# Two graph layers and two feed-forward blocks on one core: GpSimd waits for its gathers after every sixteenth

## The reference

```
h = x @ w_nbr;  agg = segment_sum(edge_weight * h[src], dst)      # first layer
x = x + agg + x_norm @ w_own + bias
x = x + mixture(x_norm)          # router, best 2 of 8 experts, gelu MLP 256 -> 1024 -> 256
for i in range(3):               # three convolutions
    h = x @ W[i];  h = segment_sum(h[src] * norm, dst) + b[i]
    x = relu(layernorm(h) * gamma[i] + beta[i])
x = x + attention_over_slices(x_norm)
```

## Time and profile before

| | us |
|---|---|
| median of 3 runs | 3794.12 (3790.35 to 3794.98) |
| profiled execution, span from first to last instruction | 4365.6 |
| prologue, to the first gather | 60.8 |
| gathers of the first layer, first to last start | 60.8 to 1212.5 |
| gathers of the three passes, first to last start | 2395.6 to 4183.6 |
| TensorE busy | 3253.1 (75%) |
| GpSimd busy | 2531.6 (58%) |
| VectorE, ScalarE busy | 1790.8 (41%), 1496.2 (34%) |

### The profile page before, as it was taken

The page is one execution under the profiler, slowest core; times in us unless marked ns, Lnnn a source line. Parts: engine busy times, 40 slices in busy tenths (PEclk is TensorE's granted clock), DMA queues, the critical chain, the costliest instruction groups (busy, mean ns, idle before and its releaser), DMA issues. The chain is left out here.

```text
span 4365.6 us, 47498 instructions
## 1 busy us (share of the span) xinstructions
PE 3253.1 (75%) x15077; PEld 2484.5 (57%) x15077; DVE 1790.8 (41%) x5335; ACT 1496.2 (34%) x2892; POOL 2531.6 (58%) x2604
## 2 busy tenths in 40 slices
PE   1455565555446989988886798987989868999868
PEld 1344444444335777776764576655666645666547
DVE  4355565534353111111117333343333435676664
ACT  3233333323323112121115244443444434555520
POOL 6666666666643656565546666665666656666620
PEclk6677777777767999999988899988999979999978
DMA  6343334334312545554437454554544534555452
GB/s 194 111 122 109 117 115 118 116 108 120 101 40 98 176 157 179 172 185 156 157 124 269 124 146 136 149 159 116 144 138 142 166 107 143 150 153 152 135 175 103
DMA packets 396972, 609.34 MB, mean 140 GB/s; under 512 B 81648, under 2 KB 295319, under 8 KB 395943
## 3 DMA queue, kind: packets, MB, share of 16 engines
q0 software_dynamic: 115808, 279.40, 22.6%
q1 hardware_dynamic: 274182, 317.02, 22.4%
q10 hardware_dynamic: 6720, 9.74, 0.7%
HBM read 509.58 MB, written 96.33 MB: 139 GB/s over the span
## 5 line engine op out<-in xcount | busy, mean ns | idle before, releaser
L2983 POOL DMA_INDIRECT rows_h<-table,step_src x1138 | 1105.8, 972 | 688.6 <-issue 342.5
L3025 PE MATMUL bank_g<-rows_hl,counts_h 128*128 128x512 f32 x3773 | 1049.8, 422 | 89.0 <-issue 45.4
L975 POOL DMA_INDIRECT rows_r<-table,step_src x782 | 749.6, 959 | 405.2 <-issue 214.1
L3025 PEld LDWEIGHTS bank_g<-rows_hl,counts_h 128*128 128x128 f32 x3773 | 721.3, 194 | 301.9 <-issue 101.0
L1000 PE MATMUL bank_r<-rows_r,hots_r 128*128 128x257 f32 x1564 | 473.4, 457 | 457.4 <-ACT rows_r L985 227.3
L1000 PEld LDWEIGHTS bank_r<-rows_r,hots_r 128*128 128x128 f32 x1564 | 340.1, 227 | 567.6 <-ACT rows_r L985 261.6
L3184 ACT ACTIVATE counts_h<-piece_h 128x896 fp32r<-128x896 uint8 x539 | 498.1, 945 | 458.8 <-PE bank_g L3025 223.3
L1901 POOL DMA_INDIRECT kept_A<-one_d,place_d x424 | 420.7, 992 | 127.4 <-issue 127.1
L2016 PE MATMUL pY_e<-w_e,h_e 128*128 128x256 f32 x1680 | 421.7, 410 | 76.7 <-ACT h_e L1982 54.4
L1011 DVE TENSOR_SCALAR hots_r<-lane,step_dst 128x128 f32<-128x128 f32 x782 | 210.3, 289 | 593.3 <-remote 365.2
L1982 ACT ACTIVATE h_e<-pH_e,prm_e 128x256 f32<-128x256 f32 (+1 forms) x456 | 179.6, 455 | 733.7 <-PE pH_e L2005 486.5
(11 more groups left out here) (397 smaller groups left out, 3864.9 us busy)
## 6 DMA issues: line engine op xcount, KB each, us to landing
w_e<-in_L_ffn_W SPq DMA_DIRECT2D x114, 1024.0 KB
piece_h<-kept_A SPq DMA_DIRECT2D x539, 112.0 KB
kept_A<-zero_r SPq DMA_DIRECT2D x189, 112.0 KB
rows_h<-table,step_src POOLq DMA_INDIRECT x1138
table<-ACC SPq DMA_DIRECT2D x51, 256.0 KB
kept_sw<-vec_g SPq DMA_DIRECT2D x49, 256.0 KB
rows_r<-table,step_src POOLq DMA_INDIRECT x782
b_e<-in_L_ffn_b SPq DMA_DIRECT2D x57, 128.0 KB
```

Source lines behind the costliest of these rows:

```text
L975: nc.gpsimd.indirect_dma_start(out=r["rows"][:, x, 0:D], out_offset=None, in_=r["table"][:, :], in_offset=bass.IndirectOffsetOnAxis(ap=c[" ...
L2983: nc.gpsimd.indirect_dma_start(out=d["rows"][:, x, :], out_offset=None, in_=tables[l - 1][:, :], in_offset=bass.IndirectOffsetOnAxis(ap=c[ ...
L3025: mm = pe.matmul(sums, d["counts"][:, n % CV, x % PC, :], both.both(t), start=(x == 0 and i >= RINGED[l]), stop=(x == NT - 1))
```

## The change

Two waits are added to GpSimd's queue and nothing else is altered. Before gathers 16, 32, 48, ... of the first layer, and before gathers 16, 32, ... of each pass, GpSimd now also waits until the gather before has landed, together with the others of its group of four slots. That is 48 places in the first layer and 22, 22 and 26 in the passes, 118 in all.

```diff
+BURST = 16
@@ run_pool
         if k % Q == 0 and k >= R:
             g.wait_ge(r["s_mm"], k - R + Q)
+        if k % BURST == 0 and k > 0:
+            g.wait_ge(r["s_row"][(k - 1) % R // Q], 16 * landed(k - 1, ET, R, (k - 1) % R // Q))
         nc.gpsimd.indirect_dma_start(
@@ layers_hybrid, block.gpsimd
                     if i % GB == 0 and i >= RG:
                         g.wait_ge(r["s_mm"], ET + earlier(l)[1] + (i - RG) // GB + 1)
+                    if i % BURST == 0 and i > 0:
+                        y = (i - 1) % RG // Q
+                        g.wait_ge(r["s_row"][y], 16 * (landed_before(l, y) + landed(i - 1, p.GT, RG, y)))
                     nc.gpsimd.indirect_dma_start(
```

## The result

The changed kernel takes 4025.6 us (4021.4 to 4030.8, 4 runs) against 3794.6 us (3790.4 to 3799.2). The ratio is 1.0608 with a 95% interval of 1.0595 to 1.0621: 231 us slower. The forecast was 3796 us with a range of 3786 to 3840.

A forecast was written before the change was run, and what follows sets the result against it. The prediction took TensorE, ScalarE and VectorE as the bound, with GpSimd ahead of them. It added 0 for the first layer and 1.6 + 0.65 + 0 for the passes: 3794.1 + 2.3 = 3796.4 us, range 3786 to 3840.

The forecast's parts named there:

- What bounds the kernel: Whole kernel: TensorE, ScalarE and VectorE bound it; GpSimd runs ahead with 162.6 us slack in the first layer, 260.2 in passes.
- Nobody waits for a gather: First layer: ScalarE waits for gathers 13 times, all before 140 us, and never in the 725 gathers after.
- GpSimd is hidden: Whole kernel: GpSimd's added waits are covered by its slack, so the time stays the same; chance 0.64.
- First layer, 48 conditions at 0: First layer: slack at the ring and TensorE's lag hide all 48 conditions, cost 0, at most 4.8 us.
- were none covered: First layer: if slack hid none of the 48 conditions, they would cost 48 x 1.6 = 77 us.
- The unit of 1.6 us: Price of one condition with GpSimd at full pace: 1.9 us from issue's end to landing, less the usual 0.3; up to 2.1.
- Passes, 70 conditions at 2.3 us: Passes: waits for TensorE cover nearly all; only 1.6 us at pass 1's end and 0.65 in pass 2 remain.
- Rival A: Without a profile GpSimd is nearly the bound, so first layer and passes 1 and 2 slow: about +50 us, 3844; chance 0.25.
- point of decision: GpSimd becomes the bound where TensorE's 16 steps take under 21.6 us; the first layer's trace has 23.6.
- The extreme of all 118 conditions uncovered: First layer and passes: GpSimd has no slack, every condition costs 1.6 us, +189 us; given no chance of its own.
- Rival B: Passes: less competition for the 16 DMA engines lets dense pieces arrive and convert earlier, -21 us, 3773; chance 0.07.
- The estimate of 2.3 us from issue to landing: One 128 KB gather: fixed 2.0 us plus bytes / 436e3 from issue's start; a condition would then cost 1.05 us.

The follow-up runs named there:

- second profile: The kernel before, with no edit, profiled again; ratio 0.9998 (0.9988 to 1.0009), profiled span 3787.9 us.

## Why the prediction was wrong

*What bounds the kernel.* This step failed, and all else with it. It took the first profile's 162.6 + 260.2 us of waits for TensorE as slack that the runs have too. The second profile has 26.5 - 87 x 0.30 = 0.4 us in the first layer and 77.3 - 46 x 0.30 = 63.5 us in the passes. GpSimd is the bound of the first layer (46 gathers fewer brought 57.4 us) and level with TensorE in the passes, so a stop of GpSimd is not hidden but paid. "Nobody waits for a gather" from 140 us on the earlier trace rows became 176 waits of ScalarE in that stretch. The first profile was 571.5 us longer than the runs; the prediction named this, and then gave the reading "GpSimd is hidden" a chance of 0.64 all the same.

*First layer, 48 conditions at 0.* They cost 118 us. The term "were none covered" had 48 x 1.6 = 77 us; nothing is covered, and the unit is 2.7 us.

*The unit of 1.6 us.* It was read between a gather's issue and ScalarE's start on it, which is 1.92 us; less 0.3. ScalarE's wake-up is no measure for GpSimd's: on one landing ScalarE started at 657.75, GpSimd at 658.49. Alone on its gather the drain adds 2.4 - 0.3 = 2.1 us, which the prediction had as its upper end, and with a blocking wait instruction in front 2.7 us. That two conditions on one gather become two instructions, the order of the change didn't show, since it prints both on one row; the count of instructions does.

*Passes, 70 conditions at 2.3 us.* They cost 109 us. "Each condition coincides with one of these waits" was read off one group of the slower execution. In the second profile, pass 2 has 5.8 us of such waits in two places.

*Rival A* (0.25) had the mechanism, but not the size: about +50 us where 231 came. Its base was close: it put the first layer at 1001 us of issuing and the passes at 472, 469 and 570, where the second profile has 991, 473, 457 and 596. Two of its terms failed. It priced a drain at 1.6 us, and it spent a lead of 30 us and "a group's lead" before charging anything, though an engine that is the bound has no lead. With 2.7 us and no lead the first layer alone gives 48 x 2.7 = 130 us; in the profiles its gathers took 1118.2 - 990.7 = 127.5 us longer. And it let everything but GpSimd shrink by one factor and stop there; its own point of decision, 21.6 us per 16 steps, was passed: 16 steps take 20.3 us in the second profile, GpSimd's own pace.

*The chances.* The objection to A, that what slows all others by 13% will hardly leave GpSimd as it is, was argued and is refuted by one row of each profile: 946 ns a gather in both. The extreme of all 118 conditions uncovered, "+189 us, nothing of its own", was nearest to the time, though by a unit too small and with nothing covered, where in fact some 70 us of the passes' pauses were. Rival B, faster by less competition, found nothing for it: the waits of TensorE for converted pieces, 42.1 us in the earlier trace rows, are 17.0 us in the second profile of the kernel before and 14.8 us after.

*The rules drawn from the Trainium skill.* The rule of the Trainium skill's "Perfetto Trace Analysis", section "Optimizing DMA Performance", that a kernel whose issuing engine's track is solid DMA slices is bound by that sequencer, was set aside on the strength of 216 pauses. In the second profile the first layer's track is solid, a gather about every 1.25 us without a stop, and this case's runs agree with the rule there (57.4 us for 46 gathers). In the passes the track has 46 waits for TensorE, and 64 gathers fewer brought 7 to 14 us. The estimate of 2.3 us from issue to landing, worked out from "DMA: Bandwidth & Descriptors", section "Anatomy of one DMA — SWDGE (gpsimd) path" of the Trainium skill, is below the 2.8 us measured (median; 2.6 to 2.7 the fastest).

## What to carry to other kernels

Compare the profile's span with the runs before anything else. Where they differ by more than a few per cent, slack read from the profile is slack of another execution; work out at once which engine would be the bound in the time that the runs have (here 782 x 1.25 us = 977 us of GpSimd against a first layer of about 1000), and give that case the weight, or the whole forecast, until something speaks against it.

Here the engine that issues the transfers was the bound of the first layer, and it paid for every drain in full: the rest of the landing plus its own restart. If such a condition is needed, ask for the landing some issues later, where it has come by itself (two gathers later cost 3 us for 118 conditions instead of 231), and where it may block, keep it the only condition of its instruction.

## What the runs showed of the hardware

- One indirect gather of 128 rows of 1 KB costs GpSimd 0.95 us, and the next starts 0.30 us later (median 946 ns in both profiles of the kernel before, though TensorE got through 12% fewer products in one); removing 46 of them from a stretch bound by GpSimd brought 57.4 us.
- A gather lands 2.8 to 2.9 us (median) after its issue starts, 6.2 us at the longest. Stopping for it makes a pause of 2.3 to 2.4 us (mean of the first layer) when the next gather holds the condition alone, and of 3.0 us when there is a second condition and so a wait instruction in front; from landing to restart it is 0.26 us against 0.76 us in most cases.
- The same separate wait instruction, when its condition is already fulfilled, costs nothing that 117 of them show (ratio 0.9999, 0.9990 to 1.0008).
- One execution of the kernel before, the one profiled first, took 4365.6 us with 12% fewer dense products a microsecond on TensorE and unchanged gathers on GpSimd; the other runs of the same program lie between 3786 and 3801 us. Its cause stays open.
